# A decoder layer with causal attention: head passes by blocks of 64 queries, weighed in pairs, and another order of a phase's work

## The chip, the cores and the metric

The kernel runs on one core of a Trainium2 chip. Its time is the device time of one execution, in microseconds (us). The engines are TensorE (PE in the profile; PEld are its weight loads), VectorE (DVE), ScalarE (ACT), GpSimd (POOL) and SyncE (SP), which issues the DMA transfers.

## The reference, cut to what matters

The input x is 8 sequences of 128 tokens with 512 channels. The first attention has 32 query heads and 8 key and value heads of 128 channels; its weights are 4-bit integers with a scale for each group of 128 rows:

```python
q = _dequant_matmul(hidden_states, qw_q, scales_q).reshape(b, s, NH, HD).transpose(0, 2, 1, 3)
k = _dequant_matmul(hidden_states, qw_k, scales_k).reshape(b, s, NKV, HD).transpose(0, 2, 1, 3)
v = _dequant_matmul(hidden_states, qw_v, scales_v).reshape(b, s, NKV, HD).transpose(0, 2, 1, 3)
q = _apply_rope(q, cos, sin)
k = _apply_rope(k, cos, sin)
scores = jnp.einsum('bhqd,bhkd->bhqk', q, k) / math.sqrt(HD)
causal = jnp.tril(jnp.ones((s, s), dtype=bool))
scores = jnp.where(causal[None, None], scores, jnp.finfo(scores.dtype).min)
attn = jax.nn.softmax(scores.astype(jnp.float32), axis=-1).astype(q.dtype)
ctx = jnp.einsum('bhqk,bhkd->bhqd', attn, v)
return _dequant_matmul(ctx, qw_o, scales_o)
```

A layernorm, a cross attention whose softmax runs over the batch, a second layernorm, a gated mixture of low-rank experts with a dense product, and a third layernorm follow. The change doesn't touch them.

## The kernel before

**Passes.** The first attention is done in 16 head passes: pass p treats key/value head p // 2 for half p % 2 of the tokens, 4 of the 8 blocks of 128 tokens. A pass has six tiles c: 0 is the key, 1 the value, 2 to 5 the four query heads that share it. Each tile is four group products G (`project`), one for each 128 input channels, G0 to G23 in all: `w_sb` times `x_hi` and `x_lo`, two f32r matmuls of 512 columns. ACT reads the first product of a tile out of PSUM with its scale (`scale_group`), DVE adds the other three (`add_group`).

**Rotary embedding.** For tiles 0 and 2 to 5, SP copies the tile with its halves exchanged (`turn`), POOL multiplies by cosine and sine and adds (`times_cos`, `times_sin`, `rotate`). The sum is written to `k_t` or `q_t`, and the scores of the pass wait for it (`rotated`). In every second phase POOL also converts the six integer weight tiles of the next head (`convert`), between these.

**Attention of one block n.** `scores` (S) multiplies four heads' queries by the 128 keys, four f32 matmuls of 128 columns into one of two PSUM banks, where ACT has put the causal mask (`seed_mask`). DVE takes the maxima, ACT the exponentials with their sums (`exps`), DVE the reciprocals (`inverse`), ACT the normalised probabilities (`normalise`). PE transposes them, four 128x128 tiles (`turn_probs`, T) into bank 5, ACT copies them out (`copy_probs`), PE multiplies by V (`weigh_v`, W, one f32 matmul of 512 columns into bank 6), ACT copies the result as f32r (`copy_heads`), DVE writes the rest (`cut_heads`). In the profile an f32 matmul is two passes, and has two records.

**Output products.** O0 to O15 (`project_out`) multiply `heads_hi` and `heads_lo` by the output weights; ACT and POOL take every fourth (`scale_out`, `add_part`), DVE adds the rest (`add_out`). G and O products share four PSUM banks in the order of the list `PRODUCTS`: each product waits until the one four places ahead has been read.

**Phases.** Phase f computes the group products of pass f + 1, the attention of the 4 blocks of pass f and the output products of pass f - 1. Each engine has the phase's steps in an order written out by hand (`phase(f)` in the block of each engine), and waits on semaphores. Phases 0 to 14 run so; a last block with a list of its own does pass 15 and starts the cross attention. Bank 5 is also used to transpose V (`turn_v`, V); the list `TURNS` says who used it last:

```python
TURNS = "V T0 T1 T2 T3".split()
```

## Time and profile before

| | |
|---|---|
| median of 3 runs | 679.2 us (676.06 to 680.47) |
| profiled execution | 676.55 us, span of the instructions 674.8 us |
| PE busy | 639.5 us (95%) |
| DVE busy | 556.5 us (82%) |
| ACT busy | 465.8 us (69%) |
| POOL busy | 420.9 us (62%) |
| granted TensorE clock | 0.992 of full speed |

The time of an execution is taken from outside the core and the span from its first to its last instruction, so the two differ a little. Busy is the time in which at least one instruction of the engine was running. Matmuls overlap in the array: the record of one is longer than the distance to the start of the next, and it is this distance (the pitch) that adds up to time. A row of the timeline that ends in x8 is eight instructions in a row.

### The profile page before, as it was taken

Reading aid. Unit: us, or ns where it says so; the run is one execution under the profiler, and the core shown is the slowest. Engines: PE = TensorE matmul, PEld = TensorE weight load, DVE = VectorE, ACT = ScalarE, POOL = GpSimd, SP = SyncE. Lnnn points to the kernel's source line nnn. Section 1 sums busy time; section 2 is a strip of 40 time slices with the busy share of each in tenths; the row PEclk is TensorE's granted clock in tenths of the full one; section 3 lists DMA queues with packets and bytes.
Section 4 is the critical chain, followed back from the end, with each engine's and each line's share of the span. In section 5 each row is a group of like instructions: output and inputs, shape, how many; then the busy total and the mean of one; then the engine's idle time right before and its main releaser. Section 6 shows DMA issues by size and latency. Waiting matters only on the chain.

```text
span 674.8 us, 11004 instructions
## 1 busy us (share of the span) xinstructions
PE 639.5 (95%) x3294; PEld 444.9 (66%) x3294; DVE 556.5 (82%) x880; ACT 465.8 (69%) x1271; POOL 420.9 (62%) x372
## 2 busy tenths in 40 slices
PE   8989999999999999999999999998998999978996
PEld 4566787877878777787777877765565444447552
DVE  5878999998999999999899989974462968998357
ACT  6697887979779797797977979776644545622100
POOL 2478899899899989989989998881230000012003
PEclk9999999999999999999999999999999998999998
DMA  7864523533351351253234124240010000020003
GB/s 232 261 166 114 154 69 96 151 109 94 110 141 46 88 165 33 59 153 90 60 111 132 43 61 114 89 127 0 1 63 0 1 1 1 0 98 2 0 1 124
DMA packets 30187, 56.72 MB, mean 84 GB/s; under 512 B 4784, under 2 KB 5040, under 8 KB 29616
## 3 DMA queue, kind: packets, MB, share of 16 engines
q1 hardware_dynamic: 30128, 56.02, 29.4%
q8 instruction: 27, 0.44, 0.3%
q14 instruction: 32, 0.26, 0.1%
HBM read 32.93 MB, written 2.10 MB: 52 GB/s over the span
## 4 chain that ended last, share of the span: by engine, by line
PE 76%; DVE 9%; ACT 4%; issue 3%; POOL 3%; DMA 2%; SPq 1%; POOLq 0%; DVEq 0%; ACTq 0%
PE ps L1527 23%; PE ps L1589 18%; PE ps L1570 8%; PE ps L1542 8%; PE ps L1597 6%; PE ps L1552 4%; PE ps L1880 3%; DMA arena<-in_qkv 2%; DVE arena L1386 2%; ACT arena L993 1%; PE ps L1770 1%; DVE arena L1359 1%; DVE late L1354 1%; DVE late L1367 1%; PE ps L1871 1%
## 5 line engine op out<-in xcount | busy, mean ns | idle before, releaser
L1140 DVE SCALAR_TENSOR_TENSOR arena<-ps,arena 128x512 f32<-128x512 f32 x288 | 212.5, 745 | 15.7 <-PE ps L1527 3.8
L1527 PE MATMUL ps<-x_hi,w_sb 128*128 128x512 f32 x384 | 170.9, 445 | 5.1 <-ACT arena L790 2.2
L1527 PE MATMUL ps<-x_lo,w_sb 128*128 128x512 f32 x384 | 150.8, 393 | 0.0
L1168 DVE SCALAR_TENSOR_TENSOR y<-ps,arena,y 128x512 f32<-128x512 f32 x192 | 138.2, 744 | 12.6 <-PE ps L1589 8.5
L799 ACT ACTIVATE arena<-ps,small 128x128 f32<-128x128 f32 x256 | 90.7, 378 | 31.3 <-DVE small L1146 26.8
L624 POOL TENSOR_TENSOR arena<-arena,consts 128x512 f32<-128x512 f32 x75 | 96.9, 1291 | 22.7 <-DVE arena L1140 22.7
L1589 PE MATMUL ps<-heads_hi,wo_sb 128*128 128x512 f32 x256 | 108.7, 425 | 0.1
L630 POOL TENSOR_TENSOR arena<-arena,consts 128x512 f32<-128x512 f32 x75 | 96.8, 1290 | 12.6 <-DMA arena<-arena 10.4
L749 POOL TENSOR_SCALAR var_eps<-mean_var 128x2 f32<-128x2 f32 (+1 forms) x13 | 7.3, 561 | 154.4 <-DVE mean_var L1278 154.4
L1589 PE MATMUL ps<-heads_lo,wo_sb 128*128 128x512 f32 x256 | 101.0, 395 | 0.0
L640 POOL TENSOR_TENSOR arena<-arena 128x512 f32<-128x512 f32 x75 | 96.6, 1287 | 5.6
L648 POOL TENSOR_TENSOR y<-arena,y 128x512 f32<-128x512 f32 x64 | 82.6, 1290 | 26.6 <-ACT arena L840 24.5
L1527 PEld LDWEIGHTS ps<-x_hi,w_sb 128*128 128x128 f32 x384 | 72.2, 188 | 39.0 <-DVE arena L1140 8.7
L790 ACT ACTIVATE arena<-ps,arena 128x512 f32<-128x512 f32 x96 | 66.6, 694 | 34.1 <-PE ps L1527 33.5
L1527 PEld LDWEIGHTS ps<-x_lo,w_sb 128*128 128x128 f32 x384 | 72.5, 189 | 16.5 <-issue 5.5
L816 ACT ACTIVATE arena<-arena,small 128x128 f32<-128x128 f32 x256 | 82.6, 419 | 0.2 <-DVE small L1152 0.2
L1570 PE MATMUL ps<-arena 128*128 128x512 f32 x128 | 66.2, 599 | 4.3 <-ACT arena L823 2.2
L1542 PEld LDWEIGHTS ps<-arena 128*128 128x128 f32 x512 | 66.2, 193 | 5.7 <-issue 1.9
L1542 PE MATMUL ps<-arena 128*128 128x128 f32 x512 | 68.0, 276 | 0.5 <-POOL arena L640 0.5
L1159 DVE TENSOR_TENSOR heads_lo<-ps,heads_hi 128x512 fp32r<-128x512 f32 x64 | 44.1, 689 | 24.4 <-ACT heads_hi L832 23.9
L1589 PEld LDWEIGHTS ps<-heads_hi,wo_sb 128*128 128x128 f32 x256 | 48.5, 189 | 16.7 <-DVE heads_lo L1159 5.6
L799 ACT ACTIVATION_READ_ACCUMULATOR arena<-ps,small 128x1 f32 x256 | 55.8, 218 | 0.0
(146 smaller groups left out, 967.6 us busy)
## 6 DMA issues: line engine op xcount, KB each, us to landing
arena<-arena SPq DMA_DIRECT2D x160, 128.0 KB, 2.3
arena<-in_qkv SPq DMA_DIRECT2D x48, 256.0 KB, 3.9
arena<-in_o SPq DMA_DIRECT2D x32, 256.0 KB, 3.7
arena<-in_x_t SPq DMA_DIRECT2D x8, 256.0 KB, 3.7
y<-in_x SPq DMA_DIRECT2D x4, 512.0 KB, 4.4
arena<-in_ctx_t SPq DMA_DIRECT2D x8, 256.0 KB, 3.1
out<-y SPq DMA_DIRECT2D x8, 256.0 KB, 2.1
arena<-in_wk SPq DMA_DIRECT2D x1, 1024.0 KB, 5.2
```

The costliest lines, as they stand in the source:

```text
L624: nc.gpsimd.tensor_tensor(by_tile(raw_cos[:, i % 2, :]), by_tile(raw[:, c % RING, :]), every_tile(cos_of(c)), ALU.mult).then_inc(cos_done, 1)
L630: nc.gpsimd.tensor_tensor(by_tile(turned[:, i % 2, :]), by_tile(turned[:, i % 2, :]), every_tile(sin_of(c)), ALU.mult).then_inc(sin_done, 1)
L640: nc.gpsimd.tensor_tensor(dst, raw_cos[:, i % 2, :], turned[:, i % 2, :], ALU.add).then_inc(rotated, 1)
L648: nc.gpsimd.tensor_tensor(dst, by_tile(out_part[:, k % 2, :]), dst, ALU.add).then_inc(part_added, 1)
L799: last = nc.scalar.activation(probs[:, s, h, :], score_ps[s][:, h * P:(h + 1) * P], ACT.Exp, bias=neg_max[:, s, h:h + 1], accum_out=row_su ...
L816: last = nc.scalar.activation(probs[:, s, h, :], probs[:, s, h, :], ACT.Copy, scale=row_inv[:, s, h:h + 1])
L1140: nc.vector.scalar_tensor_tensor(acc, group_bank(p, KC * c + g), scale_of(p // 2, c, g), acc, ALU.mult, ALU.add).then_inc(dve_scaled, 1)
L1168: nc.vector.scalar_tensor_tensor(dst, by_tile(out_bank(p, u)), out_scale_of(p // 2, u), dst, ALU.mult, ALU.add).then_inc(out_added, 1)
L1527: mm = nc.tensor.matmul(group_bank(p, u), w_sb[:, c, g, :], part[:, g, half * HALF:(half + 1) * HALF], start=(k == 0), stop=(k == 1))
L1542: mm = nc.tensor.matmul(score_ps[s][:, h * P:(h + 1) * P], q_t[:, h, b * P:(b + 1) * P], k_t[:, b * P:(b + 1) * P], start=False, stop=(n > ...
L1570: nc.tensor.matmul(pv_ps[:, :], v_sb[:, b, :], probs_t[:, s, :, :].rearrange("p h q -> p (h q)"), start=True, stop=True).then_inc(pv_done, 1)
L1589: mm = nc.tensor.matmul(out_bank(p, u), wo_sb[:, h, nt * P:(nt + 1) * P], part[:, half, h, :], start=(k == 0), stop=(k == 1))
```

## The change

Queries are taken in causal blocks of 64. Queries 0 to 63 of a block of 128 tokens only need keys 0 to 63. `q_t` is laid out so that a stationary tile holds 64 queries of two heads. Two matmuls of a block have the later 64 queries against 128 keys, two the earlier 64 against 64 keys. A block's scores fill 384 columns instead of 512, and so do mask, exponentials and probabilities. In every second block the two halves of the tokens are exchanged (in x as it is laid out, and in the tables of cosine and sine, which double in width), so that the short probabilities of two neighbouring blocks stand side by side and are transposed together: an even block has two transposes, an odd one four. `scales` and `out_scales` get places of their own.

V is weighed by pairs of blocks. Two matmuls use the full array, 256 columns each. Two more have only 64 rows of contraction, one in the upper and one in the lower half of the array. The second block's result goes to bank 5, the bank of the transposes.

GpSimd converts all six weight tiles of a head, as before. The order of a phase's steps changes on PE, ACT, DVE and POOL, and with it the lists `PRODUCTS` and `TURNS`.

```diff
-    "G0 G1 G2 O0 G3 G4 G5 G6 O1 G7 G8 G9 G10 G11 O2 O3 O4 O5 G12 O6 O7 O8 G13 G14 G15 O9 G16 G17 G18 G19 G20 "
-    "G21 O10 O11 G22 G23 O12 O13 O14 O15").split()
+    "G0 G1 G2 G3 G4 O0 G5 G6 G7 O1 G8 G9 G10 G11 G12 O2 G13 O3 G14 G15 G16 O4 G17 G18 O5 O6 O7 O8 G19 G20 O9 "
+    "G21 G22 G23 O10 O11 O12 O13 O14 O15").split()
...
-TURNS = "V T0 T1 T2 T3".split()
+TURNS = "V T0 T1 W0 T2 T3 W1".split()
...
-        consts = sb("consts", [P, 6, P])
-        ident = consts[:, 0, :]
+        consts = sb("consts", [P, 2 * P + 8 * P])
+        ident = consts[:, 0:P]
...
-        pv_ps = banks[6]
+        pv_ps = [banks[6], banks[5]]
+
+        def heads_of(n):
+
+            return pv_ps[n % 2].rearrange("p (l h q) -> p h l q", l=2, q=LOW)
...
+                if TURNS[at][0] == "W" and body >= 0:
+                    wait(nc.tensor, heads_ready, BPH * body + 2 * int(TURNS[at][1:]) + 2)
+                    return
...
-                dst = (k_t if c == 0 else q_t[:, c - 2, :])[:, half * HALF:(half + 1) * HALF]
-                nc.gpsimd.tensor_tensor(dst, raw_cos[:, i % 2, :], turned[:, i % 2, :], ALU.add).then_inc(rotated, 1)
+                dst = by_block(k_t[:, half * HALF:(half + 1) * HALF]) if c == 0 else q_out(c - 2, half)
+                nc.gpsimd.tensor_tensor(dst, by_block(raw_cos[:, i % 2, :]), by_block(turned[:, i % 2, :]),
+                                        ALU.add).then_inc(rotated, 1)
...
                 cosine(0)
                 weights(0)
                 sine(0)
+                total(0)
                 weights(1)
-                total(0)
                 cosine(2)
                 weights(2)
                 outs(3)
+                weights(3)
                 sine(2)
+                total(2)
+                sine(3)
+                cosine(3)
                 outs(7)
-                cosine(3)
-                total(2)
-                weights(3)
-                sine(3)
+                cosine(4)
                 total(3)
-                cosine(4)
...
-                for h in range(QPK):
-                    last = nc.scalar.activation(probs[:, s, h, :], score_ps[s][:, h * P:(h + 1) * P], ACT.Exp,
-                                                bias=neg_max[:, s, h:h + 1],
-                                                accum_out=row_sum[:, s, h:h + 1])
+                for i in range(QPK):
+                    last = nc.scalar.activation(probs_part(n, i), score_ps[n % 2][:, score_part(i)], ACT.Exp,
+                                                bias=neg_max[:, s, i:i + 1],
+                                                accum_out=row_sum[:, s, i:i + 1])
...
-                nc.vector.tensor_reduce(neg_max[:, s, :], score_ps[s][:, :].rearrange("p (h k) -> p h k", k=P),
+                nc.vector.tensor_reduce(neg_max[:, s, 0:2], bank[:, 0:2 * P].rearrange("p (h k) -> p h k", k=P),
+                                        AX.X, ALU.max, negate=True)
+                nc.vector.tensor_reduce(neg_max[:, s, 2:4], bank[:, 2 * P:SC].rearrange("p (h k) -> p h k", k=LOW),
                                         AX.X, ALU.max, negate=True).then_inc(max_done, 1)
...
-                for h in range(QPK):
-                    mm = nc.tensor.matmul(score_ps[s][:, h * P:(h + 1) * P], q_t[:, h, b * P:(b + 1) * P],
-                                          k_t[:, b * P:(b + 1) * P], start=False, stop=(n >= 2 or h == QPK - 1),
+                for i in range(QPK):
+                    low = i >= 2
+                    queries = q_blocks[:, b, b % 2 if low else 1 - b % 2, i % 2].rearrange("p m q -> p (m q)")
+                    keys = k_t[:, low_tokens(b) if low else slice(b * P, (b + 1) * P)]
+                    mm = nc.tensor.matmul(bank[:, score_part(i)], queries, keys, start=False, stop=(n >= 2 or i == QPK - 1),
                                           skip_group_check=(n >= 2))
...
-                for h in range(QPK):
-                    mm = nc.tensor.transpose(turn_ps[:, h * P:(h + 1) * P], probs[:, s, h, :], ident)
+                for i in range(2):
+                    mm = nc.tensor.transpose(turn_ps[:, i * P:(i + 1) * P], probs_part(n, i), ident)
+                if n % 2:
+                    for i in range(2, 4):
+                        mm = nc.tensor.transpose(turn_ps[:, i * P:(i + 1) * P], probs_low(n, i), ident)
...
-            def weigh_v(n):
-                s, b = n % 2, n % NB
-                wait(pe, probs_t_ready, n + 1)
-                wait(pe, heads_ready, n)
+            def weigh_v(pair):
+
+                n = 2 * pair
+                wait(pe, probs_t_ready, n + 2)
+                wait(pe, heads_ready, n - 1)
                 if n % BPH == 0:
                     wait(pe, v_ready, n // BPH + 1)
-                nc.tensor.matmul(pv_ps[:, :], v_sb[:, b, :], probs_t[:, s, :, :].rearrange("p h q -> p (h q)"),
-                                 start=True, stop=True).then_inc(pv_done, 1)
+                for i in range(2):
+                    nc.tensor.matmul(pv_ps[i][:, 2 * P:4 * P], v_sb[:, n % NB + i, :], probs_t[:, 2 * P * i:2 * P * (i + 1)],
+                                     start=True, stop=True)
+                for i in range(2):
+                    rows = slice(LOW * i, LOW * (i + 1))
+                    mm = nc.tensor.matmul(pv_ps[i][:, 0:2 * P], v_sb[rows, n % NB + i, :], probs_t[rows, 4 * P:6 * P],
+                                          start=True, stop=True)
+                mm.then_inc(pv_done, 1)
...
-            outs_before(9, 10)
-            cut_heads(n)
+            outs_before(9)
             inverse(n + 2)
             maxima(n + 3)
...
-            scale_out(LAST - 1, 11)
+            copy_probs(n + 1)
+            exps(n + 3)
             copy_k2(1)
             copy_heads(n)
```

On TensorE, in the second half of a middle phase, where a weighing and the third block's transposes (T2) stand. L1570 is the weighing, L1552 the transposes, L1589 an output product (its two matmuls), L1527 a group product. Before:

```order
L1527 MATMUL ps<-x_lo,w_sb 128x512
L1589 MATMUL ps<-heads_hi,wo_sb 128x512
L1589 MATMUL ps<-heads_lo,wo_sb 128x512
L1570 MATMUL ps<-arena 128x512
L1552 MATMUL ps<-consts,arena 128x128 x4
L1589 MATMUL ps<-heads_hi,wo_sb 128x512
L1589 MATMUL ps<-heads_lo,wo_sb 128x512
```

Of the changed kernel, from the weighing of the first two blocks (L1628 the full matmuls, L1632 those on half the array) to T2 (L1605); L1578 is a group product, L1652 an output product:

```order
L1628 MATMUL ps<-arena 128x256 x2
L1632 MATMUL ps<-arena 128x256 x2
L1578 MATMUL ps<-x_hi,w_sb 128x512
L1578 MATMUL ps<-x_lo,w_sb 128x512
L1578 MATMUL ps<-x_hi,w_sb 128x512
L1578 MATMUL ps<-x_lo,w_sb 128x512
L1652 MATMUL ps<-heads_hi,wo_sb 128x512
L1652 MATMUL ps<-heads_lo,wo_sb 128x512
L1578 MATMUL ps<-x_hi,w_sb 128x512
L1578 MATMUL ps<-x_lo,w_sb 128x512
L1578 MATMUL ps<-x_hi,w_sb 128x512
L1578 MATMUL ps<-x_lo,w_sb 128x512
```

The transposes stood right behind a weighing of another block; now the weighing of blocks 0 and 1 is five products (G19, G20, O9, G21, G22) ahead of T2, which waits for the two cuts of this weighing and for block 2's probabilities.

On ScalarE, the same place, in a phase with conversions of the output weights. L832 copies a block's heads, L790 evacuates a group product, L816 normalises a block, L808 writes a mask, L823 copies transposed probabilities, L799 are exponentials. Before:

```order
L816 ACTIVATE arena<-arena,small 128x128 x4
L861 ACTIVATE wo_sb<-arena 128x512
L832 ACTIVATE heads_hi<-ps 128x4x128
L790 ACTIVATE arena<-ps,arena 128x512
L816 ACTIVATE arena<-arena,small 128x128 x4
L808 ACTIVATE ps<-consts 128x512
L823 ACTIVATE arena<-ps 128x512
L790 ACTIVATE arena<-ps,arena 128x512
L799 ACTIVATE arena,small<-ps,small 128x128 x4
L832 ACTIVATE heads_hi<-ps 128x4x128
```

And in the changed kernel (L847 exponentials, L888 an output product's evacuation, L909 an output weight's conversion, L881 the heads' copies, L838 a group product's evacuation, L865 normalising):

```order
L847 ACTIVATE arena,small<-ps,small 128x64 x2
L888 ACTIVATE arena<-ps,out_scales 128x512
L909 ACTIVATE wo_sb<-arena 128x512
L881 ACTIVATE heads_hi<-ps 128x4x128 x2
L838 ACTIVATE arena<-ps,scales 128x512
L865 ACTIVATE arena<-arena,small 128x128 x2
L865 ACTIVATE arena<-arena,small 128x64 x2
L865 ACTIVATE arena<-arena,small 128x128 x2
L865 ACTIVATE arena<-arena,small 128x64 x2
```

The copies of both blocks' heads and the evacuation of G20 (tile 5) now stand between the weighing and the normalisation of block 2; the normalisations of blocks 2 and 3 follow each other.

## Rows read from the trace of the kernel before

**Rows 1.** The page: span, busy time (share) of engines, chain that ended last by engine
```profile
span 674.8 us, 11004 instructions
PE 639.5 (95%) x3294; PEld 444.9 (66%) x3294; DVE 556.5 (82%) x880; ACT 465.8 (69%) x1271; POOL 420.9 (62%) x372
PE 76%; DVE 9%; ACT 4%; issue 3%; POOL 3%; DMA 2%; SPq 1%; POOLq 0%; DVEq 0%; ACTq 0%
```
**Rows 2.** Stretches: length, busy us of PE, PEld, DVE, ACT, POOL; clock, DMA, GB/s
```profile
280.04:308.05 28.01, 28.01 (x142) 21.82 (x141) 26.12 (x43) 23.39 (x73) 24.67 (x22) 1.00 0.46 130
308.05:336.57 28.52, 28.50 (x142) 21.61 (x141) 26.34 (x43) 24.73 (x76) 27.12 (x24) 1.00 0.24 58
```
**Rows 3.** The chain that ended last, a middle phase: start us, us, what
```profile
327.77 1.85 PE ps L1527 x8
```
**Rows 4.** Timeline of PE: start us, us, line, operation, shape, count: weighing, transposes, scores
```profile
301.76 1.02 PE L1570 MATMUL ps<-arena 128*128 128x512 f32 x2
302.62 0.60 PE L1552 MATMUL ps<-consts,arena 128*128 128x128 f32 x4
302.98 0.47 PE L1589 MATMUL ps<-heads_hi,wo_sb 128*128 128x512 f32 x1
303.29 0.39 PE L1589 MATMUL ps<-heads_lo,wo_sb 128*128 128x512 f32 x1
...
312.17 1.05 PE L1542 MATMUL ps<-arena 128*128 128x128 f32 x8
312.98 0.47 PE L1527 MATMUL ps<-x_hi,w_sb 128*128 128x512 f32 x1
```
**Rows 5.** One line's instructions, the expert counts: duration ns, first and last start
```profile
L1941 PE MATMUL ps<-late,ones x16: 179/262/263, 644.3 to 645.9; 128*128 128x16 f32 x16
```
**Rows 6.** Timeline of PE in the cross attention: matmuls with 32 rows and one row
```profile
518.51 2.07 PE L1739 MATMUL ps<-w_area,arena 32*128 32x128 f32 x64 [0.69 <-ACT arena L981]
...
568.03 3.70 PE L1753 MATMUL ps<-arena 128*128 128x512 f32 x8
571.66 1.12 PE L1749 MATMUL ps<-late,ones 1*128 1x512 f32 x2
572.71 0.70 PE L1753 MATMUL ps<-arena 128*128 128x512 f32 x1
```
**Rows 7.** Timelines of DVE and POOL: a cut, a maximum, a sine product, a sum
```profile
298.41 0.68 DVE L1159 TENSOR_TENSOR heads_lo<-ps,heads_hi 128x512 fp32r<-128x512 f32 x1
299.01 0.74 DVE L1140 SCALAR_TENSOR_TENSOR arena<-ps,arena 128x512 f32<-128x512 f32 x1
...
285.31 0.68 DVE L1146 TENSOR_REDUCE small<-ps 128x4 f32<-128x512 f32 x1
285.90 0.74 DVE L1140 SCALAR_TENSOR_TENSOR arena<-ps,arena 128x512 f32<-128x512 f32 x1
...
309.12 1.29 POOL L630 TENSOR_TENSOR arena<-arena,consts 128x512 f32<-128x512 f32 x1
```
**Rows 8.** Timelines of PE and ACT: the last weighing, the copy behind it, ACT's pitches
```profile
307.59 1.02 PE L1570 MATMUL ps<-arena 128*128 128x512 f32 x2
...
308.65 0.60 ACT L832 ACTIVATE heads_hi<-ps 128x512 fp32r<-128x512 f32 x1 [0.17 <-PE ps L1570]
...
297.40 0.60 ACT L832 ACTIVATE heads_hi<-ps 128x512 fp32r<-128x512 f32 x1
297.89 0.68 ACT L790 ACTIVATE arena<-ps,arena 128x512 f32<-128x512 f32 x1
298.46 1.27 ACT L816 ACTIVATE arena<-arena,small 128x128 f32<-128x128 f32 x4
```
**Rows 9.** POOL's last sum before S0; the page's DMA rate in 40 slices
```profile
310.55 1.28 POOL L640 TENSOR_TENSOR arena<-arena 128x512 f32<-128x512 f32 x1
...
GB/s 232 261 166 114 154 69 96 151 109 94 110 141 46 88 165 33 59 153 90 60 111 132 43 61 114 89 127 0 1 63 0 1 1 1 0 98 2 0 1 124
```
**Rows 10.** Timeline of PE in the last block: a weighing and its wait
```profile
468.42 1.12 PE L1570 MATMUL ps<-arena 128*128 128x512 f32 x2 [2.15 <-ACT arena L823]
```

350 lines of the change are left out of this document (189 added, 161 removed).

## The prediction, on record before the change was run

> **What bounds the kernel now.** The profile's head first: TensorE (PE) shows matmuls in 95% of the 674.8 us span, VectorE (DVE) 82%, GpSimd (POOL) 62%, and the chain that ended last runs 76% through PE [rows 1]. A busy share can hide waits, so next the busy time by stretch, in two middle phases: 28.01 and 28.52 us long, PE busy throughout, DVE 26.1 and 26.3, POOL 24.7 and 27.1 [rows 2]. PE bounds these phases, with DVE and POOL 1.4 to 3.3 us behind. Phases 1 to 14 are 14 of this kind: half the time saved in one counts 14 times.
>
> Then the pitch of PE's work, start to start in its timeline. Eight f32r passes (four products of 512 columns) take 1.85 us, 0.46 per product [rows 3]. Weighing one block with V is one f32 matmul that runs as two passes, 301.76 to 302.62, 0.86 us; its four transposes take 0.36 plus 0.08 that the next product loses (its pass lasts 0.31 instead of 0.23), 0.44, so 0.11 each; eight score passes take 0.81 and cost the next product the same 0.08, 0.89 us [rows 4]. A phase's work is 40 products (18.3), 4 score blocks (3.56), 5 groups of four transposes (2.19) and 4 weighings (3.42): 27.5 us. So 0.5 us of an odd phase and 1.0 of an even one (the one that also converts weights) is waiting: that is all a better order can give, beside what the arithmetic gives.
>
> **The change on PE, part by part, per phase.**
>
> *Scores.* Two of a block's four heads' worth of columns now have 64 keys, so four of eight passes are half as long. The load of the stationary 128x128 tile stays. Sixteen matmuls with only 16 moving columns start between 644.3 and 645.9: 1.6 us over 15 steps, 0.107 each [rows 5]. A 128-column pass starts every 0.10 to 0.11 us [rows 4]. The short passes therefore cost what the long ones do: the saving is 0 (bounds: 0, and half the streaming of 16 passes, 0.85 us, if loads were free; I take 0, the row is of the same load).
>
> *Transposes.* Three per block on average instead of four: 4 x 0.11 = 0.43 us saved.
>
> *Weighing.* A pair of blocks cost 1.71 us. Now two full matmuls of 256 columns: 4 passes of 0.213, 0.85 us. Then two with 64 rows of contraction, on the upper and lower half of the array. That the parts of the array run side by side is shown by the 64 passes with 32 rows: 2.07 us with the last one's tail of 0.27, so 0.028 each against 0.107 alone: all four parts at once [rows 6]. For two halves I take 2 x 0.213 = 0.43 us (bounds: 0.43 and, one after the other, 0.85). But a change of partition is not free. Where eight full passes are followed by a one-row matmul, 568.03 to 571.66 is 3.63 us for 8 x 0.427 = 3.42, and the two one-row passes then take 1.04 for 0.85 before full passes resume: 0.21 + 0.20 = 0.41 us for going there and back [rows 6]. The pair costs 0.85 + 0.43 + 0.41 = 1.69 us: 0.02 saved, 0.04 a phase. The Trainium skill says the same in "TensorEngine Tiling (Array Packing)", Key Properties: a change of tiling mode drains the engine. Its section Theoretical Speedup promises up to 2x for a contraction of 64, which taken alone would make the pair 1.28 us and the phase 0.8 us shorter; by the rows the changes of mode eat this.
>
> PE's own work becomes 27.5 - 0.43 - 0.04 = 27.0 us.
>
> *What the other engines do.* DVE's maximum is split in two reductions over 384 instead of 512 elements; its 512 took 0.68 us and the next started 0.60 after it; two fixed parts more and a quarter of the elements less: -0.1 to +0.1 us each, I take 0. ScalarE (ACT) loses a quarter of the elements of exp, normalise, mask and probability copies: under 2 us a phase, on an engine with idle time; worth nothing by itself. POOL has the same 15 rotary operations and the six conversions (in both kernels; only their order changes), now with runs of 64 in the sums: 1.28 us for a contiguous sum and 1.29 for a product by tiles [rows 7, 9], so I take no change.
>
> **The new waits.** `pv_ps[1]` is bank 5, the bank of the transposes. So T2 waits until both blocks of the first weighing are copied (ACT) and cut (DVE), and in ACT's queue both copies and the evacuation of G20 stand ahead of the normalisation that T2 also needs. Count from the end of the first weighing's streaming. ACT starts 1.06 us after such a matmul pair starts, that is 0.2 after its 0.86 of streaming [rows 8]. Two copies of 0.49 end the pitch at 1.2. G20 ends at 0.2 + 0.92 + 0.17 = 1.3; its evacuation takes 0.57, the normalisation 1.27 less about 0.1 for the 64-wide ones [rows 8]: T2 can start at 3.1. DVE's path (second copy ends at 1.3, the cut 0.68 to 2.0; with (4,3) and the first cut ahead, 2.8) is shorter [rows 7]. PE arrives after the switch and five products: 0.2 + 2.3 = 2.5. **T2 waits 0.6 us in each phase.** Behind it stand G23 and all of the phase's tail. Before, the transposes of a block followed a weighing without a wait [rows 4].
>
> At a phase's start O0 now comes after five group products instead of three. It waits for G1's bank, which DVE frees after two cuts (0.60 each) and an accumulation: 0.15 us late, and 0.4 in even phases, where the fourth conversion of the output weights stands before the evacuation of O15 and so delays G0's. Three more bank waits of about 0.1 (O3, G18, O13) come from DVE, whose work of 26 us hardly shrinks. Sum: 0.6 + 0.15 + 0.3 = 1.05 us of waiting in odd phases, 1.3 in even. A phase takes 28.05 and 28.3, against 28.01 and 28.52: **0.1 us gained on average, 1.4 in 14 phases.**
>
> *S0 and GpSimd.* S0 comes one product (0.46 us) earlier. POOL's last sum ended at 311.83, S0 started at 312.17 [rows 4, 9]: 0.34 us of cover in an even phase. As the phases hardly shrink and total(0), sine and cosine stand earlier in POOL's list, I cost this at 0; uncovered it is 0.1 us per phase, 1.4 in all.
>
> *Ends.* The constants grow from 6 to 10 tables of 128 columns, by 256 KB; early on the DMA moved 232 to 261 GB/s [rows 9], so what is queued behind lands up to 1.0 us later; I take 0.7. In phase 0 POOL bounds the first scores of phase 1, so PE's saving there is lost. In the last block W0 waited 2.15 us for the probabilities' copy [rows 10]; this copy now stands before the exponentials, but W0 needs the second block's copy too, and the first layernorm statistics move behind the last two cuts. I take 0.5 saved in arithmetic and nothing from the waits (bounds: 2 us either way).
>
> **Sum.** -1.4 + 0.7 - 0.5 = -1.2 us. The profiled execution took 676.55, so 675.4. The median of the three runs, 679.2, is 2.65 higher; against it the forecast is **678**.
>
> **Rivals.**
> 1. *The waits overlap.* The order of the weighing is such that DVE and ACT catch up while PE waits for T2, and the other waits (0.45 and 0.7) and half of T2's vanish. For it: DVE has 2 us of slack in a phase [rows 2]. Then a phase is 27.3 to 27.6, 0.65 to 0.95 less than 28.25: -9 to -13, less the 0.7: 669. Against: T2's wait comes from ACT's chain, not from lag.
> 2. *The halves do not overlap fully.* If passes go strictly in program order, each f32 matmul being two passes on one half, the second of the first matmul overlaps only the first of the second: three slots of 0.213 instead of two; 0.21 x 31 pairs = +6.6: 685. Wholly one after the other: +13: 691. Against it the 0.028 us of rows 6. The skill's "TensorE: Matmul & The Clock Gate", Part 3, has matmuls start and end strictly in order, which would speak for three slots; that page's own gain for four row tiles is 3.07x.
> 3. *GpSimd decides (slower).* The sums written in runs of 64: place, the total(c) of each pass; price, 5 x 0.13 us a phase if each takes 10% longer. It decides from 0.34 us a phase on, where POOL's last sum passes S0's place; then +0.3 for the early S0 and +0.3 for the sums, 14 times: +8: 686.
> 4. *The change does not shorten PE's work at all*: half arrays as above, and the transposes' pitch rises to that of a load after each short group. Then 0.5 us a phase less is saved, +7: 684. Nothing in the rows speaks for it; I give it no chance of its own.
>
> **Chances.** Forecast (waits cancel the saving) 0.57; rival 1 0.23; rival 2 0.12 (half of it 685, half 691); rival 3 0.08. One per cent (6.8 us) is about what a measurement of this kernel can tell from no change. Faster by more: most of rival 1, 0.24 with the tail of the forecast. Slower by more: half of rival 2, most of rival 3, 0.14. Within: 0.62. The range reaches from rival 1's 669 to 688, between the two cases of rival 2.
>
> **What would show it.** Score passes at a pitch near 0.11 us whether 128 or 64 columns; the half-array pair 0.43 us long with 0.2 before and after; PE idle for about 0.6 us before the third block's transposes, released by ACT's normalisation; phases of 28.0 to 28.4 us. Wrong would be: short score passes at 0.06; no gap at the change of mode; a T2 that starts at once; S0 released by POOL in every phase.

## The result, and the profile after

The changed kernel takes 685.9 us (685.7 to 686.4 in 4 executions), the kernel before 678.4 beside it: a ratio of 1.011, 95% interval 1.009 to 1.014. It is slower by 7.6 us, where 678 was forecast; 685.9 lies in the range given, but a loss of over 1% had been given 0.14. The profiled execution has a span of 684.0 us against 674.8, 9.2 more.

The page's head, after (busy time of each engine, share of the span), which answers to [rows 1]:

```profile
span 684.0 us, 11225 instructions
PE 637.4 (93%) x3358; PEld 442.3 (65%) x3358; DVE 548.8 (80%) x944; ACT 449.6 (66%) x1272; POOL 421.3 (62%) x372
```

PE, DVE and ACT work less than before, POOL as much, and the kernel is longer: what grew is waiting. The same phases as in [rows 2], cut at the first group product of a phase; the first is odd, the second even:

```profile
core 0: us, PE busy (x) PEld busy (x) DVE busy (x) ACT busy (x) POOL busy (x), PEclk, DMA share, GB/s
287.54:316.62 29.08, 28.45 (x145) 21.57 (x144) 25.80 (x47) 22.58 (x73) 25.14 (x22) 1.00 0.45 133
316.62:345.15 28.53, 28.03 (x145) 21.75 (x144) 25.70 (x47) 23.60 (x75) 26.71 (x24) 1.00 0.21 50
```

Odd phases went from 28.01 to 29.08, even ones stayed at 28.5. (Before the change the record of G0 starts inside the weighing ahead of it, which moves this mark. By G0's second matmul the phases were 28.13 and 28.39, so odd ones grew by 0.95 and even ones by 0.14.) PE, which had no idle time there, now has 0.6 and 0.5 us, and more in stretched pitches. Over the whole span, from the first group product of each phase: phase 0 starts 0.54 us later and is 1.33 longer; phases 1 to 13 take 377.0 us instead of 368.1, 8.9 more; phase 14 takes 30.16 instead of 28.81, 1.35 more; the last block and all behind it take 2.9 less. Sum 9.2.

**What went as worked out.** PE's timeline around a weighing and a phase's start (an x8 row is eight passes):

```profile
284.68 0.40 PE L1652 MATMUL ps<-heads_lo,wo_sb 128*128 128x512 f32 x1
284.92 1.03 PE L1628 MATMUL ps<-arena 128*128 128x256 f32 x4
285.87 0.70 PE L1632 MATMUL ps<-arena 64*128 64x256 f32 x4
286.50 0.50 PE L1652 MATMUL ps<-heads_hi,wo_sb 128*128 128x512 f32 x1
286.84 0.40 PE L1652 MATMUL ps<-heads_lo,wo_sb 128*128 128x512 f32 x1
...
291.13 1.00 PE L1596 MATMUL ps<-arena 128*128 128x128 f32 x8
291.94 0.48 PE L1578 MATMUL ps<-x_hi,w_sb 128*128 128x512 f32 x1
```

Four full passes of 0.213 would end their pitch at 285.77; the half-array passes start at 285.87, 0.1 late. Four of them would need 0.85 one after the other; the next product starts 0.63 later, 286.50: two slots of 0.213, 0.1 between them and 0.1 behind, and another 0.11 is lost in that product's own pitch (286.50 to 286.84 instead of 0.23). The pair costs 1.69 us, as predicted to the hundredth, with both halves at once; the 0.41 for the changes is four pieces of 0.1, where the prediction had 0.2 on either side. Eight score passes take 0.81 us with 64 columns in half of them, as before [rows 4]: the short ones save nothing. Transposes and T2:

```profile
309.82 0.40 PE L1578 MATMUL ps<-x_lo,w_sb 128*128 128x512 f32 x1
310.67 0.44 PE L1605 MATMUL ps<-consts,arena 128*128 128x128 f32 x2 [0.45 <-ACT arena L865]
```

T2 starts 0.85 us behind the pass ahead of it instead of 0.23, 0.62 us of waiting, released by ACT's normalisation (L865): 0.6 was forecast.

**What did not.** The start of the odd phase, PE first, then ACT and DVE (L909 is the conversion of output weights, L888 O15's evacuation, L838 that of G0, L1191 DVE's accumulation of G1):

```profile
288.69 0.40 PE L1578 MATMUL ps<-x_lo,w_sb 128*128 128x512 f32 x1
289.06 0.50 PE L1578 MATMUL ps<-x_hi,w_sb 128*128 128x512 f32 x1
289.39 0.40 PE L1578 MATMUL ps<-x_lo,w_sb 128*128 128x512 f32 x1
289.73 0.48 PE L1578 MATMUL ps<-x_hi,w_sb 128*128 128x512 f32 x1
290.04 0.40 PE L1578 MATMUL ps<-x_lo,w_sb 128*128 128x512 f32 x1
290.58 0.47 PE L1652 MATMUL ps<-heads_hi,wo_sb 128*128 128x512 f32 x1
```

```profile
287.80 0.63 ACT L909 ACTIVATE wo_sb<-arena 128x512 fp32r<-128x512 int32 x1
288.33 0.67 ACT L888 ACTIVATE arena<-ps,out_scales 128x512 f32<-128x512 f32 x1
288.90 0.68 ACT L838 ACTIVATE arena<-ps,scales 128x512 f32<-128x512 f32 x1
...
289.69 1.61 DVE L1191 SCALAR_TENSOR_TENSOR arena<-ps,scales,arena 128x512 f32<-128x512 f32 x2 [0.46 <-ACT arena L838]
```

From G3 (289.06) to O0 (290.58) PE loses 0.8 us: G3 waits for O15's evacuation, O0 for G1's accumulation, and both stand behind the conversion in ACT's queue. Even phases lose 0.27 there. And DVE, after the two weighings of a phase (L1221 takes output products, L1212 cuts heads):

```profile
306.64 0.73 DVE L1221 SCALAR_TENSOR_TENSOR y<-ps,out_scales,y 128x512 f32<-128x512 f32 x1
308.39 0.75 DVE L1191 SCALAR_TENSOR_TENSOR arena<-ps,scales,arena 128x512 f32<-128x512 f32 x1 [1.02 <-PE ps L1578]
309.06 1.28 DVE L1212 TENSOR_TENSOR heads_lo<-ps,heads_hi 128x512 fp32r<-128x512 f32 x2
...
313.28 2.06 DVE L1221 SCALAR_TENSOR_TENSOR y<-ps,out_scales,y 128x512 f32<-128x512 f32 x3
316.35 0.75 DVE L1221 SCALAR_TENSOR_TENSOR y<-ps,out_scales,y 128x512 f32<-128x512 f32 x1 [1.01 <-PE ps L1652]
```

While PE weighs a pair (1.6 us) it makes nothing that DVE can read. DVE stands still for 1.0 us, takes one product, then has two cuts at once, 1.3 us in which it frees no product bank; and so again behind the second weighing. DVE's 25.7 us and these 2.0 make 27.7 of a phase of 28.5.

Then score block 0 (S0). Before, it waited in phase 1, 0.66 us, and once in the middle phases, 0.11 us. After, it waits 1.11 us in phase 2, 0.24 in phase 3, 0.31 in phase 6 and 0.17 in phase 8. POOL's waits for the exchanged tiles (`turn`) between 60 and 430 us, before and after (us in total, times, longest):

```profile
POOL arena L630 <- DMA arena<-arena: 8.1, 22, 0.9
```

```profile
POOL arena L676 <- DMA arena<-arena: 20.7, 28, 2.3
```

Part of this is a shift: POOL's waits for DVE's sums fell from 13.5 to 4.9 us in the same stretch, so all its waits grew from 22.2 to 29.2. The transfers themselves are no slower, 2.3 us at the median from issue to landing in both traces.

Last, the end of phase 14. The first product of the last block waits until O15 has been read, and O15's evacuation stands behind two head copies and the fourth conversion in ACT's queue: PE starts it at 462.00, 1.6 us late. Before, it started at 449.87, right behind the last weighing. In the last block itself PE stood still for 2.15 us ahead of W0 before the change [rows 10], and from 469.4 to 473.4 us it then ran at a granted clock of 0.57. In the changed kernel W0 doesn't wait (480.96, 0.23 behind the pass ahead) and the clock stays at 1.00 from 462 to 492 us. The 2.15 us and about 1.7 for the low clock (an estimate: 4 us at 0.57) are more than the 2.9 us that this part gained; other waits took some back.

### The profile page after: what moved, and what is told of

It reads as the page before. It is cut to its first block and busy times, and to the rows that moved or that the text cites. A ratio compares the mean times of both kernels' runs of the same rounds, so it can differ in the third digit from the quotient of the medians.

```text
span 684.0 us, 11225 instructions
## 1 busy us (share of the span) xinstructions
PE 637.4 (93%) x3358; PEld 442.3 (65%) x3358; DVE 548.8 (80%) x944; ACT 449.6 (66%) x1272; POOL 421.3 (62%) x372
## 5 line engine op out<-in xcount | busy, mean ns | idle before, releaser
L1191 DVE SCALAR_TENSOR_TENSOR arena<-ps,scales,arena 128x512 f32<-128x512 f32 x288 | 213.9, 746 | 36.6 <-PE ps L1578 18.6
L1578 PE MATMUL ps<-x_hi,w_sb 128*128 128x512 f32 x384 | 162.8, 424 | 6.1 <-DVE x_lo L1175 2.2
L1221 DVE SCALAR_TENSOR_TENSOR y<-ps,out_scales,y 128x512 f32<-128x512 f32 x192 | 139.0, 743 | 19.2 <-PE ps L1652 18.4
L1578 PE MATMUL ps<-x_lo,w_sb 128*128 128x512 f32 x384 | 151.3, 394 | 0.0
L1652 PE MATMUL ps<-heads_hi,wo_sb 128*128 128x512 f32 x256 | 109.1, 426 | 1.7 <-DVE arena L1191 0.8
L847 ACT ACTIVATE arena<-ps,small 128x128 f32<-128x128 f32 (+1 forms) x256 | 83.5, 343 | 38.1 <-DVE small L1199 32.8
L1652 PE MATMUL ps<-heads_lo,wo_sb 128*128 128x512 f32 x256 | 100.8, 394 | 0.0
L695 POOL TENSOR_TENSOR y<-arena,y 128x512 f32<-128x512 f32 x64 | 82.5, 1289 | 29.1 <-ACT arena L888 27.0
L686 POOL TENSOR_TENSOR arena<-arena 128x512 f32<-128x512 f32 x75 | 96.7, 1289 | 6.0
L1578 PEld LDWEIGHTS ps<-x_hi,w_sb 128*128 128x128 f32 x384 | 72.3, 188 | 33.1 <-DVE y L1221 4.6
L838 ACT ACTIVATE arena<-ps,scales 128x512 f32<-128x512 f32 x96 | 66.0, 687 | 28.2 <-PE ps L1578 25.1
L1578 PEld LDWEIGHTS ps<-x_lo,w_sb 128*128 128x128 f32 x384 | 72.6, 189 | 10.6
L865 ACT ACTIVATE arena<-arena,small 128x128 f32<-128x128 f32 (+1 forms) x256 | 72.9, 365 | 0.0
L1652 PEld LDWEIGHTS ps<-heads_hi,wo_sb 128*128 128x128 f32 x256 | 48.1, 188 | 30.0 <-issue 9.4
L1596 PE MATMUL ps<-arena 128*128 128x128 f32 (+1 forms) x512 | 64.2, 268 | 1.1 <-POOL arena L686 0.9
L847 ACT ACTIVATION_READ_ACCUMULATOR arena<-ps,small 128x1 f32 x256 | 53.6, 209 | 0.0
L1652 PEld LDWEIGHTS ps<-heads_lo,wo_sb 128*128 128x128 f32 x256 | 48.3, 189 | 7.0 <-issue 0.5
L881 ACT ACTIVATE heads_hi<-ps 128x512 fp32r<-128x512 f32 x64 | 34.9, 596 | 23.7 <-PE ps L1632 22.7
```

What stands on the lines that cost most here:

```text
L686: nc.gpsimd.tensor_tensor(dst, by_block(raw_cos[:, i % 2, :]), by_block(turned[:, i % 2, :]), ALU.add).then_inc(rotated, 1)
L695: nc.gpsimd.tensor_tensor(dst, by_tile(out_part[:, k % 2, :]), dst, ALU.add).then_inc(part_added, 1)
L838: nc.scalar.activation(raw_of(p, c), group_bank(p, KC * c), ACT.Copy, scale=scale_of(p // 2, c, 0)).then_inc(act_scaled, 1)
L847: last = nc.scalar.activation(probs_part(n, i), score_ps[n % 2][:, score_part(i)], ACT.Exp, bias=neg_max[:, s, i:i + 1], accum_out=row_sum ...
L865: last = nc.scalar.activation(part, part, ACT.Copy, scale=row_inv[:, s, i:i + 1])
L1191: nc.vector.scalar_tensor_tensor(acc, group_bank(p, KC * c + g), scale_of(p // 2, c, g), acc, ALU.mult, ALU.add).then_inc(dve_scaled, 1)
```

## The experiments

All are edits of the changed kernel (d4_before_light of the kernel before), each beside runs of the kernel before on the same chip. "Phases" are lengths in the trace from one phase's first group product to the next.

### One conversion moved: a1_convert

```diff
                 scale_groups(0)
                 scale_groups(1)
+                if f % 2 == 1:
+                    convert_wo(f // 2, 3)
...
-                weights(3)
+                if f == LAST - 1:
+                    weights(3)
                 outs(15)
```

> The changed kernel (685.9 us) with one step of ScalarE moved: the fourth conversion of the output weights, which stood at the end of an even phase ahead of O15's and G0's evacuation, now stands in the next odd phase behind the evacuation of G4. Theory: in the trace of the changed kernel the odd phases lose 0.8 us before and behind O0 and the even ones 0.3, because of this conversion (0.53 us) in ScalarE's queue; the start of an odd phase then reads as that of an even one, an odd phase takes 28.5 to 28.6 us instead of 29.05, an even one keeps 28.5, and the kernel gains 7 x 0.5 = 3.5 us: 682.4. Rival: the odd phases are longer for another reason (DVE's two last cuts, or GpSimd), the 0.5 us only turns into a wait at the next place (score 0 or G7): no phase changes by more than 0.15 us, 685 to 686.

684.6 us (683.9 to 686.4). An odd and an even phase:

```profile
286.50:315.01 28.51, 28.01 (x146) 21.73 (x145) 25.69 (x47) 22.56 (x73) 25.12 (x22) 1.00 0.47 134
315.01:343.52 28.51, 27.97 (x145) 21.73 (x144) 25.71 (x47) 23.63 (x75) 26.75 (x24) 1.00 0.21 52
```

Odd phases fell from 29.06 to 28.51, all from phase 3 on, and phase 1 from 29.33 to 28.85. The place of this one instruction cost 0.55 us in seven phases, 3.8 us, and phases 1 to 13 take 3.6 less together. The execution gained 1.3 only against 685.9: in this trace phase 0 took 28.7 us instead of 27.3, and what stands behind phase 13 took 1.2 more, while score block 0 waited 0.4 more (0.99, 0.40 and 0.85 us in phases 2, 6 and 8).

### T2's wait: a2_norm and a3_turn

```diff
+                norm(2)
                 copy_head(0)
                 copy_head(1)
                 scale_groups(5)
-                norm(2)
```

> The changed kernel with the normalisation of the third block ahead of the two head copies in ScalarE's queue (before, behind both copies and the evacuation of G20). ScalarE was idle for 0.65 us there and starts it at once; the copies start 0.4 us later. Theory: T2 is then released by DVE's second cut, about 0.35 us earlier than now, so of its wait of 0.6 us 0.25 is left, and all 15 phases are 0.35 us shorter: -5 us, 681. Rival: what T2 doesn't wait, O12 and O13 and the next start wait for DVE, which has 26 us of work in these phases: -0.1 us a phase, -1.5 in all, 684.5.

```diff
-                turn(2)
                 groups(5, 3)
+                turn(2)
                 outs(10, 11)
```

> The changed kernel with T2 one group product later on TensorE (behind G23 instead of ahead of it). Theory: G23 fills 0.46 of the 0.6 us that TensorE waits for T2, T2 itself starts when it does now, and every phase is 0.45 us shorter: 15 x 0.45 = 6.8, 679. G23 needs G20's bank, whose evacuation ends 1.3 us ahead of it. Rival: DVE's sums behind G23 and the tail bound the phase: the waits at O12, O13 and the next O0 grow by as much, and less than 0.15 us a phase is gained: 684 to 686.

a2_norm 690.4 us (687.1 to 690.9), a3_turn 689.2 (686.6 to 691.1). Both theories fell. In a2_norm the wait isn't even shorter: T2 is still 0.60 us late, now released by DVE's second cut, and even phases take 28.7. Two phases of a3_turn, the even one first:

```profile
378.12:406.63 28.51, 28.44 (x146) 21.72 (x144) 25.71 (x47) 23.61 (x75) 26.52 (x24) 1.00 0.22 52
406.63:435.70 29.07, 28.86 (x145) 21.57 (x144) 25.79 (x47) 22.57 (x73) 25.20 (x21) 1.00 0.33 85
```

The wait at T2 is nearly gone (0.15 us late, PE busy 28.44 instead of 28.0), the phase is as long as before the edit, to 0.02 us: PE loses 0.2 us at O10 and 0.2 at O11 instead, whose banks are free when DVE has read O9 and G21, and T3 starts only 0.07 us earlier in the phase than before the edit. The wait that had been foreseen exactly was not what set the phase.

### The changed kernel again: c0_after

> The changed kernel once more, nothing edited, to have it beside the next three: 685.9 as before if the runs on record are alike; up to 3 us more if the start and the transfers vary from run to run, as the first head pass seems to (phase 0 began at 26.9 to 29.1 us in five traces whose code ahead of it is the same).

689.9 us (687.8 to 690.9), with the kernel before at 678.9 on this chip: ratio 1.016 (1.013 to 1.018) for the same code. So medians of the changed kernel taken at different times differ by up to 4 us, and what follows goes by phases of the trace and by runs taken side by side (c0_after, b1, b2 and b3 are one such group). The steady phases are the same (28.48 and 29.11 us here). Of the 4.0 us between the two spans, phase 0 starts 1.4 later and is 1.0 longer, phases 1 to 13 take 1.1 more (score block 0: 1.27, 0.25, 1.22 and 0.16 us in phases 2, 6, 8 and 10), and the rest takes 0.5 more. In phase 0:

```profile
41.24 0.50 PE L1578 MATMUL ps<-x_hi,w_sb 128*128 128x512 f32 x1 [1.70 <-ACT arena L838]
...
42.40 0.49 PE L1578 MATMUL ps<-x_hi,w_sb 128*128 128x512 f32 x1
42.71 0.60 PE L1578 MATMUL ps<-x_lo,w_sb 128*128 128x512 f32 x1
43.11 0.63 PE L1578 MATMUL ps<-x_hi,w_sb 128*128 128x512 f32 x1
...
42.60:45.50 2.90, 2.90 (x9) 2.28 (x8) 2.02 (x5) 2.20 (x6) 2.66 (x4) 0.52 0.49 150
```

PE stood still until 41.24, and from 42.6 the granted clock is 0.52, the lower of TensorE's two levels, for 2.9 us: passes start every 0.43 us instead of 0.23, which costs 1.4 us. In the trace of the changed kernel on record PE stood as long (37.47 to 39.69) and kept 1.00.

### VectorE's load: b1_light_cuts and d4_before_light

```diff
-                nc.vector.tensor_tensor(heads_by_block(heads_lo[:, half, :, q]), heads_of(n),
-                                        heads_by_block(heads_hi[:, half, :, q].bitcast(F32)), ALU.subtract).then_inc(heads_ready, 1)
+                k = QPK if n < 2 * BPH else 2
+                nc.vector.tensor_tensor(heads_by_block(heads_lo[:, half, :, q])[:, 0:k], heads_of(n)[:, 0:k],
+                                        heads_by_block(heads_hi[:, half, :, q].bitcast(F32))[:, 0:k], ALU.subtract).then_inc(heads_ready, 1)
...
                 groups(5, 1, 2)
+                groups(5, 3)
                 turn(2)
-                groups(5, 3)
```

> T2 behind G23, as in a3_turn, and VectorE's cut of a block's heads made over two of the four heads from the third head pass on (the rest of heads_lo keeps old values, so the low parts of the products are wrong; only the time counts). VectorE works 4 x 0.3 = 1.2 us less in each phase, TensorE and ScalarE do what they did. Theory (VectorE's own queue between the two weighings and at the phase's start decides now: it stands still for 1.0 us behind each weighing and is late everywhere else): phases of 27.6 to 27.9 us instead of 28.5 to 29.06, 10 to 14 us less than a3_turn: 675 to 679. Rival (TensorE's order and ScalarE decide): phases shorten by 0.2 us at most, 683 or more.

683.8 us (683.1 to 686.9), 6.1 less than c0_after beside it. Even, then odd:

```profile
374.08:402.09 28.01, 27.95 (x145) 21.63 (x144) 24.71 (x47) 23.47 (x75) 26.52 (x24) 1.00 0.21 51
402.09:430.68 28.59, 28.38 (x146) 21.48 (x144) 24.73 (x47) 22.57 (x73) 25.19 (x21) 1.00 0.33 87
```

DVE works 1.0 us less, and each phase is 0.5 shorter than in a3_turn, whose place of T2 this kernel shares (28.51 and 29.07). The lighter cuts do two things at once: they take work off DVE and they free bank 5 and the heads sooner. a3_turn speaks for the first, since T2 hardly waits there; no run makes DVE lighter anywhere else. The same cuts in the kernel before:

> The kernel before the change with the same lighter cuts as b1_light_cuts (two of four heads from the third head pass on; the low parts are wrong, only the time counts). VectorE works 1.2 us less in each phase. Theory: before the change TensorE's own work bounds the phases (27.8 of 28.0 and 28.5 us), and VectorE's load is hidden: 0 to 0.15 us a phase, 676.5 to 679 where the kernel before takes 678.6. Rival: VectorE bounded the old order as much as the new one, the phases get 0.3 to 0.5 us shorter: 671 to 674.

678.1 us, ratio to the kernel before 0.998 (0.997 to 1.000). An odd and an even phase:

```profile
280.11:308.38 28.27, 28.21 (x143) 21.75 (x141) 25.60 (x43) 23.66 (x73) 24.64 (x21) 1.00 0.44 129
308.38:336.95 28.57, 28.39 (x143) 21.62 (x141) 25.39 (x43) 24.64 (x75) 26.89 (x25) 1.00 0.24 58
```

Most phases of either kind are now 28.24 to 28.28 us where they were 28.0 and 28.5: the sum of two, which doesn't hang on the mark, is the same. VectorE's load was hidden before the change and is not after it, though it works 0.3 to 0.6 us less per phase than before. What is left as the difference is when its work comes; no run shows this by itself. With light cuts in both, the steady phases of the new order reach 28.0 (in e3_light_both below) against 28.26: there the arithmetic that was taken away does show.

### The weighing in two pieces, and with full rows: b2_split and a4_full_rows

```diff
                                     start=True, stop=True)
+                between()
                 for i in range(2):
                     rows = slice(LOW * i, LOW * (i + 1))
...
-                weigh(0)
-                groups(4, 3)
+                weigh(0, lambda: groups(4, 3))
...
-                weigh(1)
-                outs(14, 15)
+                weigh(1, lambda: outs(14))
+                outs(15)
```

> T2 behind G23, and each weighing in two pieces: the two full matmuls, then one product (G19, or O14 in the second), then the two half-array matmuls. TensorE's work and its changes of mode are the same. Theory: VectorE stands still 1.0 us behind each weighing because for 1.6 us TensorE makes nothing that it can read; with a product in between it gets work 0.75 us earlier, twice a phase, and the phase follows by 0.4 to 0.8 us (its bound is then TensorE's 27.2 plus the phase's start): 675 to 681. Rival: the heads come 0.46 us later, the cuts, the third transposes and the next phase's start with them, and this eats it: 686 to 690.

689.8 us (688.1 to 691.0), as c0_after; phases 28.65 and 29.14. The rival's size holds. This run also bears on the reading above: between 60 and 430 us DVE's waits for PE's products fall from 27.1 us in c0_after to 6.5, but now it waits 13.0 for ACT's head copies ahead of its cuts, and 8.6 instead of 3.2 for ACT's evacuation. In all it waits 28.5 instead of 31.8 us, and no phase is shorter. So the 1.0 us of standing still behind each weighing is not, taken alone, what sets the phase. In a4_full_rows the half-array matmuls use 128 rows:

> The changed kernel with the two half-array matmuls of a weighing on the full array: 128 rows of contraction instead of 64, the same 256 columns and banks. The rows beside a short tile are the other block's, so the heads' first 64 queries are wrong; only the time counts. Theory (a change of mode costs 0.2 us each way): a pair of blocks was 4 full passes and one shared slot of 0.43 plus 0.3 to 0.4 of changing, 1.6 to 1.7 us; now it is 8 passes of 0.213, 1.71 us with no gap in it: 0 to 0.1 us more a pair, 0 to 0.2 a phase, 686 to 689. If instead the changes of mode are the lost gain (they cost more than the trace shows, since they also delay what follows), this kernel is faster: 0.2 us a phase or more, 683 or less. If the halves were worth what their overlap gives (0.43 a pair without any cost), it is 0.85 us a phase slower: 699.

690.7 us (689.3 to 693.4), phases 28.61 and 29.12. Leaving the half arrays costs 0.1 us in an even phase and nothing that shows in an odd one. That is within what was expected (1.71 against 1.69 us a pair); as DVE's lag covers part of what PE loses, the phases don't price it more closely.

### Score block 0 and GpSimd: b3_score_later, d1_dma, e1_gpsimd_order, e2_late_weights

```diff
                 outs(0)
-                score(0)
                 groups(1, 1)
-                score(1)
-                groups(1, 2, 3)
+                score(0)
+                groups(1, 2)
+                score(1)
+                groups(1, 3)
```

> The changed kernel with the first two score blocks of a phase one group product later on TensorE (behind G5 and G6). Theory: the first score block stands where GpSimd's last sum has just ended; in the phases in which the exchanged tile lands late it waits 0.2 to 1.1 us, 1.8 us in all between 60 and 432 us in the first trace of this kernel and up to 3.4 in others; one product later 0.46 of each of these waits is covered: -1 to -2 us, 684. The maxima come later by 0.46 us, which ScalarE's exponentials wait for, but T0 stands 11 us behind. Rival: a wait that is no longer met only moves to the phase's tail: 686.

691.4 us (690.2 to 692.6), 1.5 more than c0_after. S0 waits 1.0 us in all instead of c0_after's 2.9, as the theory has it, but each phase is 0.4 longer (28.9 and 29.5): G5 follows O0 at once, and its bank, which DVE frees, is not ready; the two score blocks between had covered that. The place of S0 is held from both sides.

```diff
-            W_PIECES = [(0, 1), (2,), (3,), (4,), (5,)]
+            W_PIECES = [(0, 1, 2), (3, 4), (5,), (), ()]
```

> a1_convert, and the integer weights of the next head are loaded earlier in the odd phase: three tiles behind the first exchanged tile, two behind the second, one behind the third, none behind the last two (it was 2, 1, 1, 1, 1). Theory: GpSimd's last sum, and with it score block 0 of some even phases, is late because the last exchanged tile lands behind one or two weight tiles; without weights in front it lands in about 2.3 us instead of 3.5, and the waits at S0 in the phases behind an odd one (0.3 to 1.3 us) go: no phase from 4 on is over 28.6 us, a1_convert's 1.4 us in phases 6 and 8 are gained and the 1 us of phase 2 in part: 682. Rival: three weight tiles behind the first tile delay the second and third exchanged tiles by as much, GpSimd is as late: 684 to 687.

692.4 us (690.7 to 693.7): the rival, and more. POOL's waits for exchanged tiles and PE's for POOL in phases 2 to 14 (the first column is the sum); then two stretches of phase 10, which took 32.97 us:

```profile
POOL arena L676 <- DMA arena<-arena: 24.9, 15, 4.8
PE ps L1599 <- POOL arena L686: 7.7, 6, 2.6
...
321.50:325.00 3.50, 0.89 (x4) 0.45 (x4) 2.16 (x3) 0.69 (x1) 3.37 (x4) 1.00 0.02 6
325.00:328.00 3.00, 3.00 (x14) 2.81 (x15) 1.18 (x3) 0.86 (x5) 2.86 (x3) 0.55 0.35 80
```

With more weight tiles in front of the second and third exchanged tile POOL stands still for 2.7 to 4.8 us once in each odd phase from 1 to 11. It doesn't catch up by the next S0. In phase 10, behind the longest of these waits, PE stands still for 2.7 us, and then runs 3 us at a granted clock of 0.55. The other direction:

```diff
-            W_PIECES = [(0, 1), (2,), (3,), (4,), (5,)]
+            W_PIECES = [(0,), (1,), (2,), (3,), (4, 5)]
```

> a1_convert with the integer weights of the next head later: one tile behind each of the first four exchanged tiles, two behind the last one (it was 2, 1, 1, 1, 1; d1_dma had 3, 2, 1, 0, 0 and S0 waited 9.0 us in all). Theory: what is in front of the second and third exchanged tiles decides when GpSimd comes through its list; one tile instead of two there takes 1 us off its wait, and S0 waits less in the phases behind odd ones: under 1 us in all, 682 to 683. Rival: the two tiles behind the last one land too late for the first conversion of the even phase, which GpSimd makes third: 685 or more.

686.2 us (684.5 to 689.3). S0 waits 2.6 us in phases 2 to 13, against 2.2 in a1_convert, and 0.8 against 0.2 in phase 14: nothing gained. The theory is wrong, and the rival's number (685 or more) is met.

> a1_convert with GpSimd's list in the order of the kernel before. Theory: the last sum waits for the last exchanged tile, whose transfer starts when the third tile's sum has freed its buffer, and the old order makes the sums of the first two tiles later; it gains nothing at S0, the waits there (1.4 us in phases 6 and 8, 1.1 in phase 2 in a1_convert) stay within 1 us: 684 to 686. Rival: the new list is what makes GpSimd late, and with the old one S0 never waits: 681 to 682.

715.1 and 718.6 us in its two fastest executions and 726.5 to 734.2 in the other three, against 684.6 for the same kernel with the new list. Neither expectation was near. Two of the largest waits from 60 to 430 us, in the execution of 726.5:

```profile
POOL y L695 <- ACT arena L888: 46.4, 18, 3.8
...
PE ps L1599 <- POOL arena L686: 23.2, 11, 2.4
```

The old list has `outs(7)` ahead of total(2), and O7 now comes later on PE. POOL stands in front of it, 3.8 us at worst, with the sums that S0 needs behind, and S0 waits 1.8 to 2.6 us in every phase from 2 to 13. So the new list was needed with the new order, and each phase hangs on POOL being through by its start.

### Tables in two transfers, and everything together: d2_tables, d3_all

d2_tables loads the first 768 columns of `consts` where all of them stood, and the queries' tables behind the last weight tile.

> a1_convert, and the constants come in two transfers: identity, mask and the keys' tables (384 KB, as large as all constants were before the change) where they stood, the queries' tables (256 KB) behind the last weight tile of the first head. Theory: the start is 0.5 to 2 us later than before the change because 256 KB more stand ahead of three weight tiles; with them behind, phase 0 starts at 26.9 to 27.3 us and the kernel is 0.5 to 1.5 us faster: 683 to 684. Rival: the queries' first product with the tables (GpSimd) now waits for them, phase 0 is longer by as much: 684 to 686.

686.2 us (685.5 to 687.3); phase 0 starts at 27.7 and is 28.8 long. It shows no gain: phase 0 starts at 27.7 and, in d3_all, 28.5 us with this edit, at 26.9 to 29.1 in the other versions, so what the larger constants cost stays open.

> The edits of a1_convert, a3_turn, d1_dma and d2_tables together. Theory: they add up where they act on different places: 3.5 us of the conversion, 1 to 2 of the weights, 0.5 to 1.5 of the tables, nothing of T2's place: 5 to 7 us less than the changed kernel on the same chip (c0_after, 689.9, or 685.9), 679 to 684, still not faster than the kernel before. If T2's wait was covered by the late start of the odd phases, it now gives 0.2 us a phase more: 677 to 681.

695.8 us (694.3 to 697.3): d1_dma's loss again (phase 10 takes 32.9), with nothing from T2: phases 11 and 13, at 28.51 and 28.53, are those of a1_convert.

### What is left when the three are taken away: e3_light_both, e4_spread_cuts

> The edits of a1_convert, a3_turn and b1_light_cuts, and GpSimd's sums over half the columns from the third head pass on (k and half the queries keep old values, so scores and outputs are wrong; only the time counts). Taken away are then: the conversion ahead of the odd phases, 1.2 us of VectorE's work and 3 us of GpSimd's in each phase. Theory: these three are all that the change lost in the middle phases; they fall to 27.6 to 28.0 us, odd and even alike, S0 waits for nothing from phase 2 on, and the start stays as it is (phase 0 and 1 2 to 3 us longer than before the change): 674 to 678. Rival: something else holds the phases, they stay at 28.2 us or more, 681 to 684.

676.9 us, ratio to the kernel before 0.997 (0.995 to 0.999). Even, then odd:

```profile
309.68:337.70 28.02, 27.97 (x146) 21.65 (x144) 24.73 (x47) 23.51 (x75) 24.13 (x24) 1.00 0.22 52
337.70:365.69 27.99, 27.94 (x145) 21.65 (x144) 24.72 (x47) 22.54 (x73) 22.52 (x22) 1.00 0.48 139
```

From phase 4 on all phases but one are 28.0 us, where before the change two took 56.5. The theory is borne out in its size; S0 still waits 0.1 to 0.5 us four times, which it said would be none. In steady phases the first two edits suffice: even ones were 28.01 in b1_light_cuts already, and a1_convert accounts for the odd ones. Phases 0 and 1 still take 57.4 us instead of 54.9.

> a1_convert, the third block's normalisation ahead of the head copies (a2_norm), T2 behind G23 (a3_turn), and in VectorE's queue O9's sum between the two cuts of the first weighing. Theory: the two cuts in one piece (1.3 us in which VectorE frees no bank) make O12 and O13 late; O9's bank is then free 0.65 us earlier, and T2, 0.46 us later and with its probabilities ready, hardly waits: 0.2 us a phase, 681.5 to 683. Rival: VectorE has the same work between the two weighings in any order, and its last sums decide: phases stay at 28.5 us, 684 to 686.

686.8 us (685.6 to 688.1), phases 28.65 (even) and 28.5 (odd): the rival's number. DVE's cuts may stand in one piece or two and the phase doesn't get shorter, which fits a bound by its work between the weighings but doesn't show it alone: the kernel also has a2_norm's edit, with which even phases were 28.7.

None of the versions that compute the whole layer is faster than the kernel before.

## Why the prediction was wrong, by its steps

The prediction added PE's own work and single waits. Three of its terms failed in the phases: the start of the odd phase behind the conversion (0.15 us forecast, 0.8 measured), PE's own work (0.2 us a phase too small) and S0, put at nothing (1.8 us in all).

- **PE's work.** Right in its parts: scores save 0 (0.81 us for eight passes), transposes 0.43 a phase, a pair of blocks 1.69 us. Its pitch of a product was too small: [rows 3] give 1.85 / 4 = 0.4625, and 40 of them are 18.5 us, not 18.3. With its other terms PE's own work before the change was 27.7, not 27.5. So an odd phase held 0.3 us of waiting and an even one 0.8, not 0.5 and 1.0: there was less to give back to a new order than the text says. Redone with this pitch its own sum is 28.25 and 28.5 for the two kinds of phase, 1.5 us lost in 14 phases instead of 1.4 gained, and 681 instead of 678. The sign of the forecast hung on this slip.
- **T2.** Its wait (0.6) and releaser were right, and the conclusion that the phase gets 0.6 longer by it was wrong: a3_turn took it away and nothing changed. What ran beside it is, by b1_light_cuts, DVE's lag.
- **Waits of about 0.1 from DVE, "whose work of 26 us hardly shrinks".** In the mechanism this step failed most. The waits were added to T2's as if each stood for itself and could be taken away for itself, with 2 us of slack in DVE (rival 1). But DVE reads what PE makes, through four banks: in the new order it stands still for 2 x 1.0 us behind the weighings and gets the cuts in pairs. b1_light_cuts puts 0.5 us a phase on its cuts, d4_before_light none before. In an even phase the added waits came out right all the same (1.25 us of late starts and stretched pitches, 1.3 forecast), and the phase is 28.5 where 28.3 was forecast, the difference being the pitch: a number that is right with a mechanism that is not.
- **O0 and the conversion.** The mechanism was named, but in the even phases and at 0.4 against 0.15, 0.25 us for the conversion. It stands at the end of an even phase and is paid at the start of the odd one: 0.8 against 0.27, because G3 waits as well as O0. a1_convert: 0.55 us in seven phases, 3.8 us. This is the largest single term, at half its size and in the wrong phase.
- **S0 and GpSimd at 0.** The cover of 0.34 us was seen. In the trace on record S0 waits in four phases, 1.8 us in all, in c0_after 2.9; d1_dma and e1_gpsimd_order show what it is worth when POOL falls behind (9 and 25 us of waiting). This was rival 3, with another mechanism than the one it was given: the sums in runs of 64 take 1.29 us (L686), as before, but POOL's waits for exchanged tiles grew from 8.1 to 20.7 us, and all its waits from 22.2 to 29.2.
- **Phase 0.** +0.5 for the start and +1.3 for the phase, where 0.7 was taken; in c0_after 1.9 and 2.35, 1.4 of it by the clock. In phase 0 no output products fill the waits around the paired weighings: the first is 1.3 us late, T2 0.9, T3 0.7, the second weighing 0.9. But two weighings waited there before the change too (1.0 and 1.3 us), so what the pairing costs in phase 0 wasn't separated.
- **Phase 14, last block and end.** The 1.35 us of phase 14, with its conversion ahead of O15, were not foreseen. Behind it -2.9 against -0.5: W0's wait and the low clock behind it went, where the prediction took nothing from the waits (its bounds were 2 us either way).

In one sum, phases 1 to 13: seven starts 3.8; the rest of a steady phase 28.51 against 28.24 on average, 13 x 0.27 = 3.5; S0 and what goes with it, about 1.4 more than before the change (S0's own waits 1.0 of it): 8.7 of the 8.9 us. The first is shown by a1_convert. The second goes away when DVE's cuts are light (b1_light_cuts, e3_light_both), and nothing goes away in the kernel before. That it comes from the pairing and not from another part of the new order is not shown: no run weighs blocks one by one in the new order, where the bank of the transposes leaves no room for it, and b2_split, which fills DVE's pause behind a weighing, gained nothing.

Rival 2 (the halves don't overlap) gives 685, near the 685.9 measured, by luck: the trace shows the full overlap. By the Trainium skill's "TensorE: Matmul & The Clock Gate", Part 3 (matmuls start and end strictly in program order), as rival 2 reads it, it would have been three slots; the trace has two, 285.87 to 286.50. By the Trainium skill's "TensorEngine Tiling (Array Packing)", Key Properties, a change of mode drains the engine; the trace agrees, with 0.1 us lost ahead of the half-array matmuls and 0.1 behind them. That 685.9 lies in the range of 669 to 688 is luck as well: its upper end came from rival 2, and nothing in the sum led there.
